# Scan stage of a two-layer metaformer: x1 added by a DMA after the states are turned, turns in one pass and earlier, softplus exponential in two halves

## The chip, the core and the metric

The kernel runs on one core of one Trainium2 chip, in float32. The metric is the device time of one launch in microseconds. The time of the kernel before is the median of three runs, 13239.91 us (13234.78 to 13243.13).

## The reference, cut to what matters

B = 64 images of 56x56 tokens (S = 3136) with C = 128 channels pass through two layers.

```python
x = x + window_attention(ln_c(x))                        # layer 0: x1
t = x1 + scan(ln_t(x1))                                  # layer 0: x2
#   Wx = batch_norm(ln_t(x1) @ W.T) over all tokens
#   step: y = sigmoid(wx_t + y @ V.T), 3136 steps in series, 64 images side by side
x = x2 + spectral_conv(ln_c(x2))                         # layer 1: x3
#   gates  = sigmoid(z @ Wf + bf + 2), sigmoid(z @ Wi + bi), delta = softplus(z @ Wd + bd) * 0.1
#   16 equal steps h = fg * (A*h) + delta*ig*(B*z), complex, elementwise
out = x3 + mixture_of_experts(ln_t(x3))
```

## The kernel before, in words

There are three stages: attention (one image after another, to about 5,200 us), the scan stage (`scan_phase`), and the experts. The scan stage works on all 64 images at once. In time it is cut into 25 chunks j of TF = 128 tokens (the last has 64). Each chunk has NO = 4 **slots** s = 0 to 3. In a slot three things go on beside each other, written out by hand in `slots()`:

- the recurrence of chunk j: 32 steps. A step is one product of TensorE (L1267, `vh` by the 64 states of the step before) and one tanh of ScalarE (L1136), in series. Every 8 steps the product with the inputs for 8 tokens (L1222) comes ahead of them;
- the gates of group oc: 16 images (OS) of chunk j-1. The states are turned (tokens to partitions) in four **quarters** q of 4 images by `turn_u`, copied from PSUM by `residual`, their moments are taken on VectorE (`statistics`, L935), the reciprocal root on POOL (L848 to L852), the normalization on ScalarE (L1152), the transposes on TensorE (L1254) and then 16 gate products (L1296) with two copies each (L1113, L1115). At the slot's end stand exponential (L1194) and logarithm (L1196) of the softplus, each with a table load where the function changes;
- the elementwise work of group o = oc-1 on VectorE (L1010 to L1071) with squares on ScalarE (L1157 to L1187).

Each slot has K = 32 positions k, one recurrence step each in a full chunk; TensorE and ScalarE run through them in order, and what stands at a position is done behind the step there. `turn_u` of the next group stands at k = 24, 26, 28, 30, the copies one later. A slot 0 has the turns of its own group at k = 0 to 3, since the chunk's states are complete only then; slot 3 has none for a next group. The normalization stands at k = 10 to 13 and the gates' copies from k = 17.

`turn_u` before makes one accumulation in PSUM of two things: x1, by a product with the identity (L1231), and half the state, by a product with half the identity `hident` (L1234). Both are float32 products, which take two passes, shown as two records. x1 comes from DRAM through `load_x1` on SP's queue into one of NX = 3 buffers X2. `residual` copies with a bias of 0.5. States are stored as 2y - 1, so x1 + half of one + 0.5 is x1 + y.

POOL's queue issues three accumulating transfers per group, all from SBUF to SBUF and 1 MB each: BX (L861), the state result (L817, `add_state`), and the input result (L825, `add_input`, one slot later, behind the landing of the state transfer). When that one has landed SP stores X2 to DRAM (L794). ScalarE's queue loads xh, the normalized x1, for the next chunk (L1086, `load_xq`).

The attention stage stores x1 and xh by images (L205, L207), in pieces of 512 bytes.

```python
for i in range(Q):
    w = pe.matmul(pY[0:tc, C * i:C * i + C], XU[c % 2][:, 0:tc, OS * s + Q * q + i], hident[:],
                  start=False, stop=True, skip_group_check=True)
w.then_inc(y_ps, 1)
```

## Time and profile before

| | |
|---|---|
| median of three runs | 13239.91 us |
| profiled execution, its own time | 13252.06 us |
| its span | 13250.1 us |
| PE / DVE / ACT / POOL busy | 76% / 77% / 69% / 39% |
| mean granted TensorE clock | 0.836 of full speed |
| DMA | 1215.93 MB in 1642383 packets |

The profile shows one execution. Shares of busy time are means over stages. The 40 slices of the page show the scan stage from the 17th to about the 34th, with VectorE at 8 tenths, TensorE at 7 and ScalarE at 6. The chain of work that ended last lies in the last stage and tells nothing of the scan. Within the scan I read the timeline of four slots. Busy times of neighbouring instructions overlap a little, so a stretch is best measured from start to start. Names: PEld is a weight load, SPq and ACTq are the queues of SP and ScalarE.

### The profile page before, as it was taken

What the parts mean: (1) busy time and instruction counts of PE and PEld (TensorE: products, weight loads), DVE (VectorE), ACT (ScalarE), POOL (GpSimd) and SP (SyncE); (2) the same over time, 40 slices, a digit from 0 to 9 for tenths busy, and PEclk for the clock granted to TensorE, in tenths of its full rate; (3) what the DMA queues carried; (4) which work ended last, traced back from release to release, by engine and by line L of the source; (5) the groups of instructions that cost most, each with busy time, mean ns of one, the idle gap of its engine ahead of it and who ended that gap; (6) DMA issues with size and microseconds to landing.
All of it is one profiled execution on the core that took longest, in us unless ns stands there. A gap on an engine that the chain in (4) does not pass through costs nothing. (4 is left out here: it accounts for less than half of the span.)

```text
span 13250.1 us, 228029 instructions
## 1 busy us (share of the span) xinstructions
PE 10057.1 (76%) x79510; PEld 7477.3 (56%) x79510; DVE 10189.2 (77%) x22622; ACT 9128.6 (69%) x21751; POOL 5150.9 (39%) x4755
## 2 busy tenths in 40 slices
PE   7888888888888886777777777777777777355544
PEld 5666666666666665555555555555555555133343
DVE  6777777777777774488888888888888889899910
ACT  6888888888888885466666666666666666476710
POOL 4444445444444443112212212222122122188866
PEclk9999999999999998677777777777777777677755
DMA  3333333333333332244444444444444444476544
GB/s 71 79 80 84 88 86 80 80 79 81 84 89 83 79 80 79 53 103 100 108 99 107 104 99 109 99 104 105 100 110 99 103 101 95 66 137 122 99 80 69
DMA packets 1642383, 1215.93 MB, mean 92 GB/s; under 512 B 65493, under 2 KB 1542168, under 8 KB 1603620
## 3 DMA queue, kind: packets, MB, share of 16 engines
q1 hardware_dynamic: 1345060, 756.57, 24.0%
q0 software_dynamic: 89088, 341.98, 14.0%
q10 hardware_dynamic: 207104, 102.79, 2.8%
q8 instruction: 649, 10.63, 0.3%
q14 instruction: 482, 3.95, 0.1%
HBM read 567.56 MB, written 325.32 MB: 67 GB/s over the span
## 5 line engine op out<-in xcount | busy, mean ns | idle before, releaser
L1267 PEld LDWEIGHTS s_pW<-s_XU,s_vh 128*128 128x128 f32 x6272 | 1414.0, 253 | 1884.9 <-ACT s_XU L1136 1574.5
L1267 PE MATMUL s_pW<-s_XU,s_vh 128*128 128x64 f32 x6272 | 1464.6, 325 | 1020.4 <-ACT s_XU L1136 1020.4
L1136 ACT ACTIVATE s_XU<-s_pW 128x64 f32<-128x64 f32 x3136 | 717.9, 229 | 1947.2 <-PE s_pW L1267 1927.7
L1296 PE MATMUL s_pG<-s_wg,s_XNT 128*128 128x384 f32 (+1 forms) x3200 | 1507.8, 560 | 15.4 <-ACT s_Z L1115 15.4
L409 ACT ACTIVATE KB<-pV,qkb 32x392 f32<-32x392 f32 x2048 | 1188.2, 580 | 25.7 <-PE pV L499 1.9
L249 POOL TENSOR_TENSOR SS<-SS,mx 128x784 f32<-128x784 f32 x512 | 768.7, 1501 | 805.7 <-DVE mx L342 805.5
L817 POOL DMA_DIRECT2D s_X<-s_f x100 | 87.1, 871 | 2190.4 <-DVE s_f L1067 2120.0
L1234 PEld LDWEIGHTS s_pY<-s_hident,s_XU 128*128 128x128 f32 (+1 forms) x3200 | 750.8, 305 | 174.4 <-issue 126.2
L257 POOL TENSOR_TENSOR XR<-XR,pbias 112x512 f32<-112x512 f32 x448 | 570.6, 1274 | 648.2 <-DMA XR<-in_x_dram 648.2
L461 ACT ACTIVATE XH<-XR,nm,rs 112x128 f32<-112x128 f32 x1792 | 731.3, 482 | 90.5 <-POOL nm L268 82.0
L507 PE MATMUL pS<-KB,QT 128*64 128x196 f32 x8192 | 793.3, 336 | 0.0
L529 PE MATMUL pV<-wq,XT 128*49 128x64 f32 x16384 | 564.6, 222 | 249.3 <-ACT KB L409 248.9
L507 PEld LDWEIGHTS pS<-KB,QT 128*64 128x64 f32 x8192 | 545.0, 137 | 352.8 <-issue 286.0
L353 DVE RECIPROCAL rc<-pO 128x16 f32<-128x16 f32 x512 | 131.3, 256 | 793.3 <-PE pO L550 793.3
L1152 ACT ACTIVATE s_f<-s_X,s_nmr,s_rst 128x128 f32<-128x128 f32 (+1 forms) x1600 | 652.9, 485 | 121.8 <-POOL s_nmr L852 121.7
L550 PE MATMUL pO<-Vb,PT 128*64 128x66 f32 x16384 | 591.5, 225 | 168.4 <-DVE gram L347 164.6
L1234 PE MATMUL s_pY<-s_hident,s_XU 128*128 128x128 f32 (+1 forms) x3200 | 716.8, 369 | 0.0
L529 PEld LDWEIGHTS pV<-wq,XT 128*49 128x49 f32 x16384 | 489.1, 124 | 368.7 <-ACT KB L409 368.2
L861 POOL DMA_DIRECT2D s_BX<-s_Dl x100 | 90.6, 906 | 1519.5 <-DVE s_Dl L929 1488.9
L1222 PE MATMUL s_pW<-s_XU,s_ws 128*128 128x512 f32 x784 | 671.1, 953 | 1.2 <-ACT s_XU L1096 1.2
L550 PEld LDWEIGHTS pO<-Vb,PT 128*64 128x64 f32 x16384 | 522.2, 137 | 256.9 <-DVE gram L347 217.9
L1663 PE MATMUL e_pT<-e_ident,e_X 112*128 112x112 f32 x1792 | 307.4, 335 | 443.9 <-ACT e_X L1599 288.6
(263 smaller groups left out, 30132.9 us busy)
## 6 DMA issues: line engine op xcount, KB each, us to landing
XL<-in_x_dram SPq DMA_DIRECT2D x64, 1568.0 KB, 12.4
XR<-in_x_dram SPq DMA_DIRECT2D x64, 1568.0 KB, 18.0
x_dram<-XR SPq DMA_DIRECT2D x64, 1568.0 KB, 8.0
xh_dram<-XH SPq DMA_DIRECT2D x64, 1568.0 KB, 8.1
e_X<-out_dram SPq DMA_DIRECT2D x64, 1568.0 KB, 16.1
s_XQ<-xh_dram ACTq DMA_DIRECT2D x384, 256.0 KB, 3.3
s_BX<-s_Dl POOLq DMA_DIRECT2D x96, 1024.0 KB, 7.0
s_X<-s_f POOLq DMA_DIRECT2D x96, 1024.0 KB, 7.0
```

The costliest lines, as they stand in the source:

```text
L249: pool.tensor_tensor(sv[:], sv[:], mx[wi % 2][:].unsqueeze(2).broadcast_to([P, 16, L]), ALU.subtract).then_inc(s_sub, 1)
L409: i = act.activation(KB[par][r, :, h, :], pV[r, 0:NW * L].rearrange("c (w l) -> c w l", l=L), ACT.Identity, bias=qkb[r, 1:2])
L461: i = act.activation(XH[q.par][:, n0, 0:C], XR[q.par][:, n0, :], ACT.Identity, bias=nm2[:, k, t:t + 1], scale=rs2[:, k, t:t + 1])
L507: i = pe.matmul(pS[64 * s:64 * s + 64, p // 2, (p % 2) * NH * L:(p % 2 + 1) * NH * L], QT[par][:, w * L:w * L + 64], KB[par][:, w, :, :].r ...
L529: i = pe.matmul(pV[64 * o:64 * o + L, 64 * w:64 * w + 64], XT[im.par][:, wi, w, :], wq[:, 2 * C:3 * C].rearrange("c (a b d) -> c a b d", a ...
L550: i = pe.matmul(pO[64 * s:64 * s + 64, hp, 66 * p:66 * p + 66], PT[par][:, p, hp, 64 * s:64 * s + 64], Vb[par][:, w, hp, :], start=True, s ...
L1136: act.activation(XU[j % 2][:, t, :], pW[t // R % 2][:, B * (t % R):B * (t % R) + B], ACT.Tanh, scale=0.5).then_inc(u_sb, 1)
L1152: w = act.activation(XN[0:tc, i, :], X2[oc % NX][0:tc, i, :], ACT.Identity, bias=nmr[0:tc, i:i + 1], scale=rst[0:tc, i:i + 1])
L1222: pe.matmul(pW[r % 2][:, 0:R * B], ws[:], XU[j % 2][:, R * r:R * r + R, :].rearrange("c t b -> c (t b)"), start=True, stop=False, skip_gro ...
L1234: w = pe.matmul(pY[0:tc, C * i:C * i + C], XU[c % 2][:, 0:tc, OS * s + Q * q + i], hident[:], start=False, stop=True, skip_group_check=True)
L1267: pe.matmul(pW[t // R % 2][:, B * (t % R):B * (t % R) + B], vh[:], before, start=False, stop=True, skip_group_check=True).then_inc(z_ps, 1)
L1296: pe.matmul(pG[i % 3][0:tc, 0:3 * C], XNT[:, i, 0:tc], wg[:], start=True, stop=True).then_inc(g_ps, 1)
```

## The change

Of the attention stage: x1 and xh are stored with the token as the outer dimension and the image as the second, so that 16 images of a token lie together (8 KB), and neighbouring tokens 32 KB apart.

Of the scan stage:

- `turn_u` is now four transposes of the states into PSUM, without x1. `hident` goes. The copy `residual` multiplies by 0.5 and adds 0.5. It waits for the store that last used the buffer.
- x1 is added to X2 afterwards by a transfer on POOL's queue from DRAM, `add_x1`, a fourth accumulating transfer per group. SP's loads go. `statistics` waits for its landing. For the groups of slots 1 to 3 it is issued in the slot before, between the BX transfer and the state transfer; for that of slot 0 in slot 0 itself, behind the input transfer of the group before.
- The turns of the next group move from k = 24, 26, 28, 30 to k = 17, 19, 21, 23, the copies from k = 25, 27, 29, 31 to k = 18, 20, 22, 24.
- The exponential is made of two halves, of 8 images each: the first at k = 29, the second at the old place.
- xh is loaded in pieces of 2 KB.

```diff
@@ -60,6 +60,11 @@
 def tokens_of(dram, b):
 
     return dram[bass.ds(b, 1)].rearrange("a (n r) w c -> (a r w) n c", r=2)
+
+
+def token_rows(dram, b):
+
+    return dram[:, b, :].rearrange("(n t) c -> t n c", t=T)
 
 
 PIECES = 1
...
@@ -202,9 +207,9 @@
                 if prev:
                     q = m.step(-1)
                     wait(sp, x1_sb, m.idx * NG)
-                    sp.dma_start(tokens_of(x1_d, q.idx), XR[q.par][:]).then_inc(x1_st[q.par], 16)
+                    sp.dma_start(token_rows(x1_d, q.idx), XR[q.par][:]).then_inc(x1_st[q.par], 16)
                     wait(sp, xh_sb, m.idx * NG)
-                    sp.dma_start(tokens_of(xh_d, q.idx), XH[q.par][:, :, 0:C]).then_inc(xh_st[q.par], 16)
+                    sp.dma_start(token_rows(xh_d, q.idx), XH[q.par][:, :, 0:C]).then_inc(xh_st[q.par], 16)
 
             bodies(body, sp)
             for i in range(2):
...
@@ -716,8 +720,9 @@
         cst = sem("cst"); ini = sem("ini"); dch = sem("dch"); pch = sem("pch"); mmc = sem("mmc")
         ready = sem("ready"); bf_d = sem("bf_d"); fold_ps = sem("fold_ps"); fold_d = sem("fold_d")
         xq_ld = [sem(f"xq_ld{i}") for i in range(2)]
-        x2_ld = [sem(f"x2_ld{i}") for i in range(NX)]
-        x3_st = sem("x3_st"); first_added = sem("first_added"); both_added = sem("both_added")
+        x1_added = [sem(f"x1_added{i}") for i in range(2)]
+        x3_st = [sem(f"x3_st{i}") for i in range(2)]
+        first_added = sem("first_added"); both_added = sem("both_added")
         d_ld = sem("d_ld"); d_ps = sem("d_ps")
         xt_ps = sem("xt_ps"); xt_sb = sem("xt_sb")
         w_ps = sem("w_ps"); z_ps = sem("z_ps"); u_sb = sem("u_sb")
...
@@ -758,6 +763,9 @@
 
         def tokens(dram, b0, n, j):
             return dram[b0:b0 + n, j * TF:j * TF + size(j), :].rearrange("b t c -> t b c")
+
+        def rows_of(dram, b0, n, j):
+            return dram[j * TF:j * TF + size(j), b0:b0 + n, :].rearrange("t b c -> t (b c)")
 
         @block.sync
         def _(sp):
...
@@ -775,15 +783,7 @@
                 sp.dma_start(kern[64:64 + L, o:o + HC], im).then_inc(cst, 16)
                 sp.dma_start(kern[64:64 + L, o + HC:o + 2 * HC], re).then_inc(cst, 16)
 
-            def load_x1(o):
-                c, s = divmod(o, NO)
-                wait(sp, x3_st, (o - NX + 1) * 16)
-                sp.dma_start(X2[o % NX][0:size(c)], tokens(x1_d, OS * s, OS, c)).then_inc(x2_ld[o % NX], 16)
-
-            load_x1(0)
             for j, s, oc, o, scan, prep in slots():
-                if oc is not None and oc + 1 < NGR:
-                    load_x1(oc + 1)
                 if scan and s == 1:
                     wait(sp, d_ps, j)
                     for n, a, e, at in pieces(j):
...
@@ -791,8 +791,9 @@
                 if o is not None:
                     c, s_ = divmod(o, NO)
                     sp.wait_ge(both_added, (o + 1) * 16)
-                    sp.dma_start(tokens(x3_d, OS * s_, OS, c), X2[o % NX][0:size(c)]).then_inc(x3_st, 16)
-            sp.wait_ge(x3_st, NGR * 16)
+                    sp.dma_start(tokens(x3_d, OS * s_, OS, c), X2[o % NX][0:size(c)]).then_inc(x3_st[o % 2], 16)
+            for i in range(2):
+                sp.wait_ge(x3_st[i], NGR // 2 * 16)
 
         @block.gpsimd
         def _(pool):
...
@@ -810,6 +811,13 @@
             pool.wait_ge(dch, 5)
             pool.tensor_tensor(fld[4], fld[3], nhalf[:, 0:C], ALU.pow).then_inc(pch, 1)
 
+            def add_x1(o):
+
+                c, s_ = divmod(o, NO)
+                pool.wait_ge(x2_d, o * NQ + NQ)
+                pool.dma_start(X2[o % NX][0:size(c)].rearrange("t b c -> t (b c)"), rows_of(x1_d, OS * s_, OS, c),
+                               accum_op=ALU.add).then_inc(x1_added[o % 2], 16)
+
             def add_state(o):
 
                 n = size(o // NO)
...
@@ -829,6 +837,8 @@
             for j, s, oc, o, scan, prep in slots():
                 if o is not None and o >= 1:
                     add_input(o - 1)
+                if oc is not None and s == 0:
+                    add_x1(oc)
                 if scan and s == NO - 2:
                     tj = size(j)
                     pool.wait_ge(raw_d, j + 1)
...
@@ -860,6 +870,8 @@
                     pool.wait_ge(bp, oc + 1)
                     pool.dma_start(BX[0:tc].rearrange("t r b c -> t (r b c)"), Dl[0:tc].rearrange("t r b c -> t (r b c)"),
                                    accum_op=ALU.add).then_inc(bx_d, 16)
+                if oc is not None and s + 1 < NO:
+                    add_x1(oc + 1)
                 if o is not None:
                     add_state(o)
             add_input(NGR - 1)
...
@@ -929,7 +940,7 @@
                 dve.tensor_tensor(Dl[0:tc], of[:, ::-1], by(C), ALU.mult).then_inc(part_sem, 1)
 
             def statistics(oc, tc):
-                dve.wait_ge(x2_d, oc * NQ + NQ)
+                dve.wait_ge(x1_added[oc % 2], (oc // 2 + 1) * 16)
                 wait(dve, ag_d, oc)
                 for i in range(OS):
                     w = dve.bn_stats(st[0:tc, i, :], X2[oc % NX][0:tc, i, :])
...
@@ -1083,7 +1094,7 @@
 
                 j, b = divmod(i, NO * NQ)
                 if j < NCH:
-                    act.dma_start(XQ[i % 2][0:size(j)], tokens(xh_d, Q * b, Q, j)).then_inc(xq_ld[i % 2], 16)
+                    act.dma_start(XQ[i % 2][0:size(j)].rearrange("t b c -> t (b c)"), rows_of(xh_d, Q * b, Q, j)).then_inc(xq_ld[i % 2], 16)
 
             def keep_turned(j, s, q):
 
...
@@ -1102,8 +1113,10 @@
 
                 tc = size(oc // NO)
                 act.wait_ge(y_ps, oc * NQ + q + 1)
+                if q == 0 and oc >= NX:
+                    act.wait_ge(x3_st[(oc - NX) % 2], ((oc - NX) // 2 + 1) * 16)
                 act.activation(X2[oc % NX][0:tc, Q * q:Q * q + Q, :].rearrange("t b c -> t (b c)"), pY[0:tc, :], ACT.Identity,
-                               bias=cols[0:tc, 1:2]).then_inc(x2_d, 1)
+                               bias=cols[0:tc, 1:2], scale=0.5).then_inc(x2_d, 1)
 
             def gate(oc, tc, i):
                 act.wait_ge(g_ps, oc * OS + i + 1)
...
@@ -1114,6 +1127,13 @@
                                scale=0.5)
                 act.copy(Z[0:tc, :, i, :], bank[:, 2 * C:3 * C].rearrange("t (r c) -> t r c", r=2)).then_inc(g_sb, 1)
 
+            def exponential(oc, tc, first, last):
+
+                act.wait_ge(g_sb, oc * OS + last)
+                if first == 0:
+                    act.wait_ge(bx_d, (oc + 1) * 16)
+                act.activation(Dl[0:tc, :, first:last], Z[0:tc, :, first:last], ACT.Exp).then_inc(sp_d, 1)
+
             for i in range(2):
                 load_xq(i)
 
...
@@ -1137,8 +1157,8 @@
                                            scale=0.5).then_inc(u_sb, 1)
                     if conv and s == 0 and k in (1, 2, 3, 4):
                         residual(oc, k - 1)
-                    if conv and s + 1 < NO and k in (25, 27, 29, 31):
-                        residual(oc + 1, (k - 25) // 2)
+                    if conv and s + 1 < NO and k in (18, 20, 22, 24):
+                        residual(oc + 1, (k - 18) // 2)
                     if prep and k in (1, 4, 7, 10):
                         keep_turned(j, s, k // 3)
                     if conv and 10 <= k < 10 + NQ:
...
@@ -1187,12 +1207,12 @@
                         act.activation(t1, t2, ACT.Square, bias=cols[0:tm, 2:3]).then_inc(am, 1)
                     if conv and k > K - OS:
                         gate(oc, tc, k - (K - OS) - 1)
+                    if conv and k == K - 3:
+                        exponential(oc, tc, 0, OS // 2)
                 if conv:
                     gate(oc, tc, OS - 1)
-                    act.wait_ge(g_sb, oc * OS + OS)
-                    act.wait_ge(bx_d, (oc + 1) * 16)
-                    act.activation(Dl[0:tc], Z[0:tc], ACT.Exp).then_inc(sp_d, 1)
-                    act.wait_ge(sp_d, oc * 2 + 1)
+                    exponential(oc, tc, OS // 2, OS)
+                    act.wait_ge(sp_d, oc * 3 + 2)
                     act.activation(Dl[0:tc], Dl[0:tc], ACT.Ln, bias=cols[0:tc, 0:1]).then_inc(sp_d, 1)
 
         @block.tensor
...
@@ -1226,13 +1246,8 @@
                 c, s = divmod(oc, NO)
                 tc = size(c)
                 wait(pe, x2_d, oc * NQ + q)
-                if q == 0:
-                    pe.wait_ge(x2_ld[oc % NX], (oc // NX + 1) * 16)
-                pe.matmul(pY[0:tc, :], ident[0:tc, 0:tc], X2[oc % NX][0:tc, Q * q:Q * q + Q, :].rearrange("t b c -> t (b c)"),
-                          start=True, stop=False, skip_group_check=True)
                 for i in range(Q):
-                    w = pe.matmul(pY[0:tc, C * i:C * i + C], XU[c % 2][:, 0:tc, OS * s + Q * q + i], hident[:],
-                                  start=False, stop=True, skip_group_check=True)
+                    w = pe.transpose(pY[0:tc, C * i:C * i + C], XU[c % 2][:, 0:tc, OS * s + Q * q + i], ident[:])
                 w.then_inc(y_ps, 1)
 
             def turn_inputs(j, s, q, oc):
...
@@ -1277,8 +1292,8 @@
                         if k == 0:
                             pe.wait_ge(u_sb, (j - 1) * TF + tc)
                         turn_u(oc, k)
-                    if conv and s + 1 < NO and k in (24, 26, 28, 30):
-                        turn_u(oc + 1, (k - 24) // 2)
+                    if conv and s + 1 < NO and k in (17, 19, 21, 23):
+                        turn_u(oc + 1, (k - 17) // 2)
                     if prep and k in (0, 3, 6, 9):
                         turn_inputs(j, s, k // 3, oc)
                     if conv and 11 <= k < 11 + NQ:
...
@@ -1709,9 +1724,10 @@
     with ExitStack() as ctx:
 
         gram = ctx.enter_context(nc.sbuf_tensor("gram", [C, C + 1], F32))
+        x1_d, xh_d = (d.rearrange("b h w c -> (b h w) c").rearrange("(s b) c -> s b c", b=B) for d in (x1_d, xh_d))
         attention_phase(nc, B, A["x"], A["w_qkvT"], A["qkv_bias"], A["w_projT"], A["proj_bias"], A["rel_table"],
                         A["mask"], A["ident"], A["ones"], x1_d, xh_d, gram)
-        scan_phase(nc, B, x1_d.rearrange("b h w c -> b (h w) c"), xh_d.rearrange("b h w c -> b (h w) c"), gram,
+        scan_phase(nc, B, x1_d, xh_d, gram,
                    A["w_ffnT"], A["v_ffnT"], A["gamma"], A["beta"], A["w_gates"], A["b_gates"], A["dft"],
                    (A["A_re"], A["A_im"]), (A["B_re"], A["B_im"]), A["ident"], A["ones"], out)
         tv_d = nc.dram_tensor("tv_dram", [2, B, E, TOPK // 2], F32, kind="Internal").ap()
```

TensorE, the later part of a slot with turns, before. s_pY<-s_X,s_ident is x1 by the identity, s_pY<-s_hident,s_XU the states, s_pG a gate, s_pW<-s_XU,s_vh a step.

```order
L1231 MATMUL s_pY<-s_X,s_ident 128x512
L1234 MATMUL s_pY<-s_hident,s_XU 128x128 x4
L1296 MATMUL s_pG<-s_wg,s_XNT 128x384
L1267 MATMUL s_pW<-s_XU,s_vh 128x64
L1296 MATMUL s_pG<-s_wg,s_XNT 128x384
L1267 MATMUL s_pW<-s_XU,s_vh 128x64
L1231 MATMUL s_pY<-s_X,s_ident 128x512
L1234 MATMUL s_pY<-s_hident,s_XU 128x128 x4
L1296 MATMUL s_pG<-s_wg,s_XNT 128x384
L1267 MATMUL s_pW<-s_XU,s_vh 128x64
L1296 MATMUL s_pG<-s_wg,s_XNT 128x384
L1267 MATMUL s_pW<-s_XU,s_vh 128x64
```

The same engine after the change, from the step of k = 17 on.

```order
L1282 MATMUL s_pW<-s_XU,s_vh 128x64
L1250 MATMUL s_pY<-s_ident,s_XU 128x128 x4
L1311 MATMUL s_pG<-s_wg,s_XNT 128x384
L1282 MATMUL s_pW<-s_XU,s_vh 128x64
L1242 MATMUL s_pW<-s_XU,s_ws 128x512
L1311 MATMUL s_pG<-s_wg,s_XNT 128x384
L1282 MATMUL s_pW<-s_XU,s_vh 128x64
L1250 MATMUL s_pY<-s_ident,s_XU 128x128 x4
L1311 MATMUL s_pG<-s_wg,s_XNT 128x384
L1282 MATMUL s_pW<-s_XU,s_vh 128x64
L1311 MATMUL s_pG<-s_wg,s_XNT 128x384
L1282 MATMUL s_pW<-s_XU,s_vh 128x64
```

Before, a turn stands among the last eight gates; now it stands among the first eight, and x1's product is not there.

POOL from the end of a slot 3 into slot 0, before (s_BX<-s_Dl is the BX transfer, s_X<-s_f the state's, s_X<-s_Wv the input's).

```order
L861 DMA s_BX<-s_Dl 128x2048
L817 DMA s_X<-s_f 128x2048
L825 DMA s_X<-s_Wv 128x2048
L848 TENSOR_TENSOR s_rst<-s_var,s_epst 128x16
L850 TENSOR_TENSOR s_rst<-s_rst,s_nhalf 128x16
L852 TENSOR_TENSOR s_nmr<-s_mean,s_rst 128x16
```

The same place after the change.

```order
L862 TENSOR_TENSOR s_nmr<-s_mean,s_rst 128x16
L871 DMA s_BX<-s_Dl 128x2048
L825 DMA s_X<-s_f 128x2048
L833 DMA s_X<-s_Wv 128x2048
L818 DMA s_X<-x_dram 128x2048
L858 TENSOR_TENSOR s_rst<-s_var,s_epst 128x16
L860 TENSOR_TENSOR s_rst<-s_rst,s_nhalf 128x16
L862 TENSOR_TENSOR s_nmr<-s_mean,s_rst 128x16
```

At the turn from slot 3 to slot 0, x1's transfer (s_X<-x_dram) stands behind the input transfer and ahead of the reciprocal roots; in the other slots it stands ahead of the state transfer.

ScalarE at a slot's end, after the change (L1135 is the exponential, L1156 the step's tanh).

```order
L1156 ACTIVATE s_XU<-s_pW 128x64
L1126 ACTIVATE s_TG<-s_pG 128x4x64
L1128 COPY s_Z<-s_pG 128x2x64
L1135 ACTIVATE s_Dl<-s_Z 128x2x512
L1156 ACTIVATE s_XU<-s_pW 128x64
L1126 ACTIVATE s_TG<-s_pG 128x4x64
L1128 COPY s_Z<-s_pG 128x2x64
L1156 ACTIVATE s_XU<-s_pW 128x64
L1126 ACTIVATE s_TG<-s_pG 128x4x64
L1128 COPY s_Z<-s_pG 128x2x64
L1126 ACTIVATE s_TG<-s_pG 128x4x64
L1128 COPY s_Z<-s_pG 128x2x64
L1135 ACTIVATE s_Dl<-s_Z 128x2x512
L1216 ACT_TABLE_LOAD
```

The first half of the exponential stands ahead of the tanh of k = 30.

## Rows read from the trace of the kernel before

**Rows 1.** Windows, scan stage: engines' busy time with counts, granted clock, DMA share, GB/s.

```profile
5000.00:11400.00 6400.00, 4805.53 (x19398) 3463.39 (x19399) 5239.44 (x5770) 4140.21 (x10445) 1440.06 (x852) 0.77 0.42 98
```

**Rows 2.** Line L1194 on ScalarE: count, ns min/median/max, first and last start.

```profile
L1194 ACT ACTIVATE s_Dl<-s_Z x100: 1909/1910/1917, 5493.8 to 11499.2; 128x2048 f32<-128x2048 f32 x96, 64x2048 f32<-64x2048 f32 x4
```

**Rows 3.** Timeline, ScalarE, slots' ends: start us, duration us, instruction [idle before <-releaser].

```profile
8010.81 1.91 ACT L1194 ACTIVATE s_Dl<-s_Z 128x2048 f32<-128x2048 f32 x1
...
8072.10 1.91 ACT L1194 ACTIVATE s_Dl<-s_Z 128x2048 f32<-128x2048 f32 x1
...
8121.62 1.91 ACT L1194 ACTIVATE s_Dl<-s_Z 128x2048 f32<-128x2048 f32 x1
...
8195.83 1.91 ACT L1194 ACTIVATE s_Dl<-s_Z 128x2048 f32<-128x2048 f32 x1
...
8256.61 1.91 ACT L1194 ACTIVATE s_Dl<-s_Z 128x2048 f32<-128x2048 f32 x1
```

**Rows 4.** Timeline, TensorE: one quarter turned, and four transposes of inputs.

```profile
8005.48 1.13 PE L1231 MATMUL s_pY<-s_X,s_ident 128*128 128x512 f32 x2
...
8006.02 2.04 PEld L1234 LDWEIGHTS s_pY<-s_hident,s_XU 128*128 128x128 f32 x8 [0.24 <-issue]
...
8007.97 0.32 PEld L1296 LDWEIGHTS s_pG<-s_wg,s_XNT 128*128 128x128 f32 x2
...
8010.05 0.57 PEld L1247 LDWEIGHTS s_pX<-s_ident,s_XQ 128*128 128x128 f32 x4
```

**Rows 5.** Tile s_XU: weight loads of the states, ns min/median/max.

```profile
L1234 PEld LDWEIGHTS s_pY<-s_hident,s_XU x3200: 184/313/338, 5429.8 to 11452.0; 128*128 128x128 f32 x181, 128*64 128x64 f32 x8
```

**Rows 6.** Windows of slot 3 around the clock's rise.

```profile
8104.00:8108.00 4.00, 4.00 (x8) 2.18 (x8) 4.00 (x4) 1.31 (x6) 0.90 (x1) 0.51 0.66 133
8108.00:8112.00 4.00, 3.67 (x17) 2.33 (x16) 1.51 (x2) 2.96 (x11) 0.00 (x0) 1.00 0.66 135
```

**Rows 7.** Timeline, VectorE, slot 3 and the start of slot 0.

```profile
8071.28 3.19 DVE L935 BATCH_NORM_STATS2 s_st<-s_X 128x6 f32<-128x128 f32 x16 [0.66 <-ACT s_X L1105]
...
8075.32 1.23 DVE L1010 TENSOR_TENSOR s_f<-s_TG 128x1024 f32<-128x1024 f32 x1
...
8099.37 2.29 DVE L928 TENSOR_TENSOR s_BX<-s_f,s_par_b 128x2048 f32<-128x2048 f32 x1 [2.33 <-ACT s_f L1152]
...
8110.89 1.23 DVE L1053 SCALAR_TENSOR_TENSOR s_f<-s_f,s_d 128x1024 f32<-128x1024 f32 x1 [2.49 <-ACT s_f L1183]
...
8113.23 1.23 DVE L1055 SCALAR_TENSOR_TENSOR s_t<-s_t,s_d 128x1024 f32<-128x1024 f32 x1 [1.11 <-ACT s_t L1187]
...
8129.65 1.23 DVE L1010 TENSOR_TENSOR s_f<-s_TG 128x1024 f32<-128x1024 f32 x1
...
8143.47 3.19 DVE L935 BATCH_NORM_STATS2 s_st<-s_X 128x6 f32<-128x128 f32 x16 [2.34 <-ACT s_X L1105]
```

**Rows 8.** Timeline, POOL and SP's queue, slot 0.

```profile
8135.69 0.86 POOL L825 DMA_DIRECT2D s_X<-s_Wv  x1 [7.35 <-DMA s_X<-s_f]
...
8142.64 0.37 SPq L794 DMA_DIRECT2D out_dram<-s_X  x1
...
8154.88 0.67 POOL L852 TENSOR_TENSOR s_nmr<-s_mean,s_rst 128x16 f32<-128x16 f32 x1
```

**Rows 9.** Window of slot 0 while POOL's input transfer runs.

```profile
8137.00:8139.00 2.00, 1.33 (x8) 1.20 (x7) 1.97 (x2) 0.63 (x2) 0.00 (x0) 1.00 0.98 197
```

**Rows 10.** DMA queues of the page: packets, MB, share of 16 engines.

```profile
q1 hardware_dynamic: 1345060, 756.57, 24.0%
q0 software_dynamic: 89088, 341.98, 14.0%
```

**Rows 11.** Timeline, slot 0: ScalarE's normalization and who reads its result.

```profile
8155.58 1.65 ACT L1152 ACTIVATE s_f<-s_X,s_nmr,s_rst 128x128 f32<-128x128 f32 x4 [3.91 <-POOL s_nmr L852]
...
8162.78 2.29 DVE L928 TENSOR_TENSOR s_BX<-s_f,s_par_b 128x2048 f32<-128x2048 f32 x1 [5.08 <-ACT s_f L1152]
```

**Rows 12.** DMA issues of the page: KB each, median us to landing.

```profile
x_dram<-XR SPq DMA_DIRECT2D x64, 1568.0 KB, 8.0
```

4 lines of the change are left out of this document (1 added, 3 removed).

## The prediction

> **What bounds the kernel now.** I read the busy times of the scan stage first. Between 5000 and 11400 us VectorE is busy 5239 us of 6400, TensorE 4806, ScalarE 4140, and TensorE has a mean clock of 0.77 [rows 1]. No engine is full, so the order between them counts. The exponential of the softplus stands once at each slot's end and serves as a mark: 100 of them from 5493.8 to 11499.2 us, 60.7 us from one to the next [rows 2]. In the chunk I read, one after the other, the slots take 61.3, 49.5, 74.2 and 60.8 us [rows 3]. These are s = 2, 3, 0 and 1, 245.8 us together. Slot 3 turns no states for a next group; slot 0 turns its own and the next group's.
>
> **TensorE's part.** One quarter of the states is turned from 8005.48, when the identity product on x begins, to 8007.97, when the next gate weights are loaded [rows 4]: 2.5 us at full clock. Four of them and what they hold up are the 11.8 us between slots 2 and 3 [rows 3]. The change drops the identity product and one of the two passes. The eight weight loads of the states take 2.04 us [rows 4], so four take 1.0 us; the longest single one is 338 ns [rows 5], so 1.3 us at half clock. Both ends of the price of a new quarter stand in rows: 0.57 us, as the four transposes of contiguous data take [rows 4], and 1.35. I take 1.0 at full clock, since the states still lie apart in memory.
>
> **Where they go.** They move from k = 24 to 30 to k = 17 to 23. There ScalarE has two squares (k = 20 and 22), behind which the turns at k = 21 and 23 lie, and now the four copies from PSUM of about 0.57 us as well. Unhidden are the turns at 17 and 19 (1.3 and 1.0) and the copies at 20, 22, 24 and part of that at 18: 4.7 us a slot. The least is 2.3 (the two turns alone), the most 6.6 (four turns and four copies).
>
> **The exponential.** 1.91 us [rows 3] become two of about 1 us. The second saves 0.95 us at the slot's end. The first stands on ScalarE in front of the step of k = 30, and that step waits for it; about 0.6 comes back. Net gain 0.35 us a slot, between 0 and 0.95.
>
> **So TensorE and ScalarE alone** would allow 49.5 - 0.35 = 49.15 us in slot 3, and 53.9 in slots 1 and 2, together 157.
>
> **VectorE is late next.** In slot 3 it goes from 8075.32 to 8129.65 with waits of 2.33, 2.49 and 1.11 us: 48.4 us of work. Statistics of a group take 4.05 (8071.28 to 8075.32) [rows 7]. Beside that I allow 1.0 and 2.4 us for the spectrum's operations in slots 1 to 2 and 2. For slots 1 to 3 that is 3 x 48.4 + 3 x 4.05 + 3.4 = 160.8 us of work. Some 2 us of waits for ScalarE's squares stay in each slot, 166.8. VectorE comes into slot 1 about 6 us behind the mark and leaves slot 3 about 8 behind (8129.65 against 8121.62 before [rows 3, 7]), so 2.2 of it fall outside: 164.6 us for three slots that took 171.6. **Gain 7.0**, at most 10.5 (without waits), at least 2.
>
> **Slot 0 pays.** Its statistics needed only ScalarE's copy and began 21.9 us after the mark (8143.47), after a wait of 2.34 us [rows 7]. Now they need the added x1. Its transfer can start only when the copies are done, about 16.4 us after the mark (0.95 from the tail and 1.5 from each of three turns, 5.4 earlier than before). But POOL issues it behind the input transfer of the group before. That was issued 14.1 us after the mark (8135.69) [rows 8] and lands about 7 us later, at 21. VectorE now comes into the slot about 0.6 us later than before: 21.7. Do the two run at the same time? During the earlier one all 16 DMA engines were busy (0.98) [rows 9]. The software queue took 14.0% of 16 engines' span for 342 MB: 5.4 us per MB; its three transfers per group carry 300 MB in all, so 6.2 us per transfer. The hardware queue took 24.0% for 757 MB, 4.2 us per MB [rows 10]. Behind the first, x1 lands at 21.7 + 6.2 = 27.9 at the earliest. As the store of the finished group starts then too (8142.64, 21.0 after the mark [rows 8]), at 21.7 + 6.2 + 4.2 = 32.1 at the latest, or 33 with a load of xh. I take 31.5, the shared end, since both are issued at the same moment. The Trainium skill, "DMA: Bandwidth & Descriptors", section on queues, rings and completion order, says that each DMA engine goes round-robin between the queue rows that have work; by that the shared end is the right one, by a strict order of arrival it would be 27.9.
>
> From there the old chain follows: from the start of statistics to the end of POOL's last operation (8155.55) 12.1 us [rows 7, 8]; ScalarE's normalization 7.2 (8155.58 to 8162.78) [rows 11]; and from there to the slot's end 33.0 [rows 3], now 33.0 - 11.3 (turns; 0.5 of the 11.8 are slot 2's spectrum) + 4.7 + 0.6 = 27.0. New length 31.5 + 12.1 + 7.2 + 27.0 = 77.8 us instead of 74.2. **Loss 3.6.** ScalarE waited 3.91 us there for POOL [rows 11]; it will wait some 19 (5.4 earlier there, 9.7 later served), with TensorE idle.
>
> **Costed at nothing.** SP's loads of x1 go; none was waited for. Loads of xh in longer pieces were hidden. The attention stage stores x1 and xh with neighbouring tokens 32 KB apart. One store of 1568 KB lands in 8.0 us [rows 12] and an image takes some 80; it would have to take nearly ten times as long to be seen. If that cover were gone, each us beyond would cost 64. POOL's wait for the copies of k = 24 stands ahead of its state transfer, which VectorE releases later anyway, and delays nothing.
>
> **Sum.** +3.6 - 7.0 = -3.4 us per chunk, 25 chunks: -85 us. The profiled execution took 13252.1 us, 12 more than the median of 13239.9; from it 13167, from the median 13155. What a measurement can tell from no change is 0.2%, 26 us or 1.1 us per chunk.
>
> **Rivals.**
> 1. *The late x1 decides (slower).* One mechanism: x1 queues behind another transfer ahead of slot 0's statistics. Each us of its landing costs 25 us. At 31.5 the kernel gains 85; at 34.9 it breaks even; from 36 on it is slower by over 0.2%. At 39, if store and xh loads come first and the transfer from DRAM has a longer way, it is 13155 + 7.5 x 25 = 13340. For it: the engines are full at that place [rows 9]. Against: the bytes queued there give 33. Chance 0.24; a shortfall of VectorE's gain to its least, 2, gives the same sign and is counted here.
> 2. *x1 slips through.* It lands at 27.9, and VectorE's waits shrink to nothing: -3.6 - 3.5 = -7.1 more per chunk, 12980. For it: transfers may overlap their fixed part. Chance 0.20.
> 3. *The clock stays low.* In slot 3 the granted clock is 0.51 from 8104 to 8108, with 8 products started, and 1.00 from 8108 to 8112, with 17 [rows 6]: half the rate is about 1 us per step and gate. It rose after a row of gate products; now transposes with the idle array between them stand there, and slot 0 idles longer ahead. If the full clock came four steps later in slots 0 to 2, slot 0 would lose 4 us, and VectorE, the later one in the others, would hide about half: +8 per chunk, 13355. The Trainium skill, "TensorE: Matmul & The Clock Gate", section on the transpose in TensorE, says that transposes do not count as busy for the clock in the way products do; by it this rival would come out. Against: slot 3 has no turns at all and reaches 1.00 by its gates alone, so I give 0.08.
> 4. *It evens out.* Gains of VectorE's slots and slot 0's loss are equal within 1.1: 13240. Chance 0.12.
>
> **Chances.** Forecast 0.36, rivals 0.24, 0.20, 0.08, 0.12. Faster takes the forecast and the second: 0.56; slower the first and third, less a little at their near edge: 0.30; the rest 0.14. The range leaves out half of the second rival's far end and the tops of the first and third: 13000 to 13320. The forecast's own range is 13080 to 13210.
>
> **What would show it.** Marks of slots 1 and 2 about 55 to 57 us apart, slot 3 about 53, slot 0 about 78. In slot 0 statistics wait for the x1 transfer and begin about 31 us after the mark, and ScalarE's normalization waits about 19 us for POOL. The turn of a quarter takes 1.0 to 1.3 us. Statistics of the other slots wait for nothing. The attention stage has the same length. I am wrong if slot 0 is not longer, or if slots 1 to 3 sum to under 160 or over 169 us.

## The result, and the profile after

The changed kernel takes **13162.5 us**, the median of four runs (13158.25 to 13164.23), against 13239.6 for the kernel before in four runs beside them: a ratio of 0.9941, 95% interval 0.9925 to 0.9957. That is 77 us less. Forecast were 13155 and a range of 13000 to 13320.

The slots' ends can be read as before. The first view is ScalarE's timeline of the kernel after: the second half of the exponential at each slot's end (start us, duration us, instruction).

```profile
7962.83 1.06 ACT L1135 ACTIVATE s_Dl<-s_Z 128x1024 f32<-128x1024 f32 x1
...
8023.98 1.06 ACT L1135 ACTIVATE s_Dl<-s_Z 128x1024 f32<-128x1024 f32 x1
...
8076.71 1.11 ACT L1135 ACTIVATE s_Dl<-s_Z 128x1024 f32<-128x1024 f32 x1
...
8150.46 1.06 ACT L1135 ACTIVATE s_Dl<-s_Z 128x1024 f32<-128x1024 f32 x1
...
8205.02 1.06 ACT L1135 ACTIVATE s_Dl<-s_Z 128x1024 f32<-128x1024 f32 x1
```

| slot | before [rows 3] | forecast | after |
|---|---|---|---|
| 2 | 61.3 | 55 to 57 | 61.2 |
| 3 | 49.5 | 53 | 52.7 |
| 0 | 74.2 | 77.8 | 73.7 |
| 1 | 60.8 | 55 to 57 | 54.6 |
| 1 to 3 together | 171.6 | 164.6 | 168.4 |
| chunk | 245.8 | 242.4 | 242.2 |

The chunk came out within 0.2 us of the forecast, by two errors of about 4 us that cancel: slot 0 was shorter than forecast, and slot 2 gained nothing. The chunk that I read is a usual one: the medians over all chunks, slots 0 to 3, are 74.2, 60.7, 61.3 and 49.5 us before and 73.7, 54.3, 61.0 and 52.7 after. From the first mark to the last the scan took 6005.4 us before [rows 2] and 5926.9 after (5495.3 to 11422.2, by the second halves), 78.5 less. The two profiled executions differ by more, 13250.1 and 13156.4 us of span. The rest lies behind the last mark, where the execution of before took 1750.9 us and this one 1734.2; the profiles of three variants (the late turns, the new layout alone, the early turns alone) have 1728.9 to 1733.5 there, so it was that one execution of before that was long, and not the change.

The next view is the windows of the kernel after, the scan stage as in [rows 1] and then slots 2, 3, 0 and 1. The columns are those of [rows 1]: length, PE, PEld, DVE, ACT and POOL busy, granted clock, DMA share, GB/s.

```profile
5000.00:11400.00 6400.00, 4167.50 (x17204) 2939.09 (x17204) 5320.54 (x5869) 4227.06 (x10652) 1642.33 (x966) 0.69 0.46 99
...
8023.98:8076.71 52.73, 35.28 (x131) 24.52 (x131) 52.08 (x61) 38.63 (x100) 8.11 (x6) 0.71 0.44 100
8076.71:8150.46 73.75, 43.65 (x175) 31.20 (x173) 53.63 (x53) 43.50 (x109) 12.09 (x8) 0.68 0.46 100
8150.46:8205.02 54.56, 40.62 (x153) 28.74 (x153) 51.80 (x52) 40.92 (x105) 9.73 (x7) 0.69 0.54 117
7962.83:8023.98 61.15, 41.21 (x157) 28.87 (x155) 53.17 (x56) 41.38 (x105) 31.19 (x13) 0.69 0.48 103
```

TensorE has lost 640 us of busy time in the stage (4805.5 to 4167.5) and the kernel only 77: TensorE is not what sets the slots now. In slot 3 VectorE is busy 52.08 of 52.73 us, and in slot 1 51.80 of 54.56. Slots 0 and 2 are the ones with idle time on VectorE, 20 and 8 us. The timeline of VectorE after, slot 3 and the start of slot 0, answers to [rows 7]:

```profile
8036.83 1.23 DVE L1021 TENSOR_TENSOR s_f<-s_TG 128x1024 f32<-128x1024 f32 x1
...
8084.98 1.23 DVE L1021 TENSOR_TENSOR s_f<-s_TG 128x1024 f32<-128x1024 f32 x1
...
8105.30 3.19 DVE L946 BATCH_NORM_STATS2 s_st<-s_X 128x6 f32<-128x128 f32 x16 [8.84 <-DMA s_X<-x_dram]
...
8124.60 2.29 DVE L939 TENSOR_TENSOR s_BX<-s_f,s_par_b 128x2048 f32<-128x2048 f32 x1 [5.09 <-ACT s_f L1172]
```

From 8036.83 to 8084.98 there is no bracket at all on VectorE: 48.15 us of pure work, where it had three waits before. Then the statistics of slot 0 wait 8.84 us for the landing of x1, 28.6 us after the mark at 8076.71. What was queued there is in the timeline of POOL, SP and ScalarE, slot 0 after, which answers to [rows 8] and [rows 11]:

```profile
8090.95 0.86 POOL L833 DMA_DIRECT2D s_X<-s_Wv  x1 [7.29 <-DMA s_X<-s_f]
8092.25 0.87 POOL L818 DMA_DIRECT2D s_X<-x_dram  x1 [0.43 <-ACT s_X L1118]
...
8099.41 0.37 SPq L794 DMA_DIRECT2D out_dram<-s_X  x1
...
8116.70 0.67 POOL L862 TENSOR_TENSOR s_nmr<-s_mean,s_rst 128x16 f32<-128x16 f32 x1
...
8117.40 1.65 ACT L1172 ACTIVATE s_f<-s_X,s_nmr,s_rst 128x128 f32<-128x128 f32 x4 [17.01 <-POOL s_nmr L862]
```

The input transfer is issued at 8090.95, x1 1.3 us behind it, the store 7.2 us later. ScalarE waits 17.0 us for POOL. x1 has moved to the software queue, which carries 444.75 MB now instead of 341.98 [rows 10]. From the page's DMA part (the second line is to be read against [rows 12]):

```profile
q0 software_dynamic: 103232, 444.75, 18.7%
...
x_dram<-XR SPq DMA_DIRECT2D x64, 1568.0 KB, 8.1
...
s_XQ<-xh_dram ACTq DMA_DIRECT2D x384, 256.0 KB, 4.5
```

### The profile page after: what moved, and what is told of

The parts are those of the page before. It is cut to its first block and busy times, and to the rows that moved or that the text cites. A ratio compares the mean times of both kernels' runs of the same rounds, so it can differ in the third digit from the quotient of the medians.

```text
span 13156.4 us, 223254 instructions
## 1 busy us (share of the span) xinstructions
PE 9385.1 (71%) x77110; PEld 6941.7 (53%) x77110; DVE 10185.1 (77%) x22621; ACT 9159.4 (70%) x21851; POOL 5332.7 (41%) x4855
## 3 DMA queue, kind: packets, MB, share of 16 engines
q0 software_dynamic: 103232, 444.75, 18.7%
## 5 line engine op out<-in xcount | busy, mean ns | idle before, releaser
L1282 PEld LDWEIGHTS s_pW<-s_XU,s_vh 128*128 128x128 f32 x6272 | 1451.6, 263 | 2039.1 <-ACT s_XU L1156 1758.7
L1282 PE MATMUL s_pW<-s_XU,s_vh 128*128 128x64 f32 x6272 | 1523.5, 336 | 1132.1 <-ACT s_XU L1156 1117.2
L1156 ACT ACTIVATE s_XU<-s_pW 128x64 f32<-128x64 f32 x3136 | 715.0, 228 | 1179.0 <-PE s_pW L1282 1146.8
L1269 PE MATMUL s_pN<-s_ident,s_f 128*128 128x128 f32 (+1 forms) x800 | 211.0, 418 | 826.1 <-issue 437.9
L437 ACT COPY Vb<-pV 49x512 f32<-49x512 f32 x1024 | 597.6, 584 | 61.7 <-PE pV L534 3.0
L1311 PEld LDWEIGHTS s_pG<-s_wg,s_XNT 128*128 128x128 f32 (+1 forms) x3200 | 561.3, 212 | 141.2 <-issue 111.2
L1126 ACT ACTIVATE s_TG<-s_pG 128x256 f32<-128x256 f32 (+1 forms) x1600 | 621.1, 388 | 9.7 <-DVE s_Wv L1046 2.4
```

What stands on the lines that cost most here:

```text
L1126: act.activation(TG[0:tc, :, i, :], bank[:, 0:2 * C].rearrange("t (r c) -> t r c", r=4), ACT.Tanh, scale=0.5)
L1156: act.activation(XU[j % 2][:, t, :], pW[t // R % 2][:, B * (t % R):B * (t % R) + B], ACT.Tanh, scale=0.5).then_inc(u_sb, 1)
L1282: pe.matmul(pW[t // R % 2][:, B * (t % R):B * (t % R) + B], vh[:], before, start=False, stop=True, skip_group_check=True).then_inc(z_ps, 1)
L1311: pe.matmul(pG[i % 3][0:tc, 0:3 * C], XNT[:, i, 0:tc], wg[:], start=True, stop=True).then_inc(g_ps, 1)
```

## Experiments

Slot lengths below are read from each run's marks as above. All kernels start from the changed one but two, which start from before (the early turns alone and the new layout alone); each ratio is against the kernel before, run beside it. The runs were made in several sets, in which the kernel before took 13231.5, 13234.9 and 13239.6 us; a difference between two variants given in us can be off by such an amount. Each trace is that of one execution.

### Slot 0: is it the late x1, and what makes it late?

**Without x1 in slot 0** (`add_x1` is not issued for the groups of slot 0, whose statistics wait for ScalarE's copies instead):

```diff
-                if oc is not None and s == 0:
-                    add_x1(oc)
...
-                dve.wait_ge(x1_added[oc % 2], (oc // 2 + 1) * 16)
+                if oc % NO == 0:
+                    dve.wait_ge(x2_d, oc * NQ + NQ)
+                else:
+                    dve.wait_ge(x1_added[oc % 2], (oc // 2 + 1 if oc % 2 else oc // NO + 1) * 16)
```

> The changed kernel without x1 for the groups of slot 0: its transfer is left out there and statistics wait for the copies alone (a quarter of the groups lacks x1). In the changed kernel statistics of slot 0 waited 8.84 us for that transfer. Theory (slot 0 pays for the late x1): slot 0 becomes some 9 us shorter, 25 times, 12940 us. Rival (VectorE is the bound over all four slots, so that a later wait takes the place): under 100 us less, 13070 or more.

12917.4 us, ratio 0.9761 (0.9745 to 0.9778). Slot 0 takes 64.3 us, and its statistics start 18.9 us after the mark. The late x1 costs 245 us, and 9.5 us in the slot 0 that I read: much more than the 3.6 that I had put down as slot 0's loss, because without it slot 0 would have gained 10.

**Slot 0 the old way** (`load_x1` on SP's queue, x1's identity product and the two-pass products in slot 0 alone; other slots as changed):

```diff
...
+                if s == 0:
+                    if q == 0:
+                        pe.wait_ge(x2_ld, (c + 1) * 16)
+                    pe.matmul(pY[0:tc, :], ident[0:tc, 0:tc], X2[oc % NX][0:tc, Q * q:Q * q + Q, :].rearrange("t b c -> t (b c)"),
+                              start=True, stop=False, skip_group_check=True)
                 for i in range(Q):
-                    w = pe.transpose(pY[0:tc, C * i:C * i + C], XU[c % 2][:, 0:tc, OS * s + Q * q + i], ident[:])
+                    if s == 0:
+                        w = pe.matmul(pY[0:tc, C * i:C * i + C], XU[c % 2][:, 0:tc, OS * s + Q * q + i], hident[:],
+                                      start=False, stop=True, skip_group_check=True)
+                    else:
+                        w = pe.transpose(pY[0:tc, C * i:C * i + C], XU[c % 2][:, 0:tc, OS * s + Q * q + i], ident[:])
...
```

> Groups of slot 0 get x1 as before the change (SP loads it, product with the identity, two passes for the states), the other three as after it. Theory: in slot 0 the four old turns put the last copy at about 21 us after the mark (21.8 before the change, less the shorter tail) instead of x1's landing at 28.6; 7.6 us less, 25 times, 12970 us. Rival (what counts in slot 0 is TensorE's own work and clock): the old turns cost there what the wait did, 13160.

12939.4 us, ratio 0.9777 (0.9761 to 0.9793). Slot 0 takes 64.6 us, its statistics start 20.6 us after the mark and wait 0.78 us. So slot 0 is as short with the old, dearer turns as with the new ones and no x1 (64.3): there it is not TensorE that counts but when x1 has arrived.

**x1 ahead of the input transfer** on POOL's queue in slot 0:

```diff
-                if o is not None and o >= 1:
-                    add_input(o - 1)
                 if oc is not None and s == 0:
                     add_x1(oc)
+                if o is not None and o >= 1:
+                    add_input(o - 1)
```

> In slot 0 POOL issues x1's transfer ahead of the input transfer of the group before, not behind it. Theory (x1 stands in a full queue): the copies are done about 15.5 us after the mark, x1 lands alone at about 23 to 24 instead of 28.6, statistics begin 5 us earlier, 13040 us. Rival (transfers in flight share the engines whatever their order): x1 lands where it did, 13160. The input transfer lands later, at about 29, which statistics cover.

12934.1 us, ratio 0.9775 (0.9759 to 0.9792). The two lines' order alone is worth 228 us, and the result is within 17 us of the kernel that has no x1 there at all. The expected 13040 was too high. Timeline of VectorE and POOL in this kernel's slot 0, whose mark is at 7977.46:

```profile
8001.07 3.19 DVE L946 BATCH_NORM_STATS2 s_st<-s_X 128x6 f32<-128x128 f32 x16 [3.80 <-DMA s_X<-x_dram]
...
8006.80 2.29 DVE L939 TENSOR_TENSOR s_Wv<-s_IN,s_par_a 128x2048 f32<-128x2048 f32 x1 [1.62 <-DMA s_X<-s_Wv]
```

```profile
8005.26 0.21 POOL L858 TENSOR_TENSOR s_rst<-s_var,s_epst 128x16 f32<-128x16 f32 x1 [10.48 <-DVE s_var L85]
8005.55 2.93 POOL L860 TENSOR_TENSOR s_rst<-s_rst,s_nhalf 128x16 f32<-128x16 f32 x1
8008.56 0.61 POOL L862 TENSOR_TENSOR s_nmr<-s_mean,s_rst 128x16 f32<-128x16 f32 x1
```

x1 lands 23.6 us after the mark instead of 28.6, the 5.0 us expected. The other 4 us are seen at POOL: its three operations end 3.9 us after they began, and VectorE now waits 1.62 us for the input transfer beside them. In the changed kernel they run beside VectorE's work and take 7.9 us (8109.49 to 8117.37), as they did before (8147.67 to 8155.55), and as they do in the run without x1, where VectorE does not wait there either. That the wait is what makes them short is read from these timelines and was not tried by itself.

**The store held back.** SP waits with the store of the finished group until slot 0's statistics are done. The first form had the group's number one off and held another slot's store, where nothing is late:

```diff
+                    if (o + 1) % NO == 0 and o + 1 < NGR:
+                        sp.wait_ge(ag_d, o + 2)
```

> In slot 0 SP stores the finished group only once the statistics are done, so that the store does not run beside x1's transfer. If the store and x1 share the engines, as I took it for the prediction: x1 lands at 27 instead of 28.6, up to 35 us less in all, 13130. If the order of arrival decides: no change, 13160.

13154.5 us, ratio 0.9942 (0.9925 to 0.9958): the same as the change. It decides nothing, and serves as a second measurement of it. The right form:

```diff
+                    if (o + 2) % NO == 0 and o + 2 < NGR:
+                        sp.wait_ge(ag_d, o + 3)
```

> The wait of e_hold stood one slot off and held no store of slot 0; here SP's store that falls in slot 0 is held until slot 0's statistics are done. If x1 and the store share the engines equally, x1 lands 3 to 4 us earlier than its 28.6 after the mark, 13070. If the earlier transfer keeps nearly all of the engines: under 1 us, 13150.

13146.3 us, ratio 0.9934 (0.9917 to 0.9950). Timeline of VectorE and SP's queue in slot 0 of this kernel, whose mark is at 8074.28:

```profile
8102.57 3.19 DVE L948 BATCH_NORM_STATS2 s_st<-s_X 128x6 f32<-128x128 f32 x16 [8.59 <-DMA s_X<-x_dram]
```

```profile
8106.75 0.37 SPq L796 DMA_DIRECT2D out_dram<-s_X  x1
```

The store is issued behind x1's landing now, and x1 lands 28.3 us after the mark instead of 28.6. So the store does not delay it. The packets of the kernel after show it too. First the queues between the store's issue and x1's landing (8099.41 to 8105.30), then from there to 8109.50 (packets, MB, share of 16 engines; q0 is POOL's, q1 SP's):

```profile
q0 software_dynamic: 125, 0.89, 77.3%
...
q1 hardware_dynamic: 128, 0.07, 4.1%
```

```profile
q1 hardware_dynamic: 1936, 0.98, 77.4%
```

Of the store's 2064 packets 128 run before x1 has landed, and 1936 after it. What delays x1 is the input transfer ahead of it on its own queue. The store, which waits for that transfer, is issued 22.7 us after the mark, and x1 lands 5.9 us behind that.

### Slot 2: why did it gain nothing?

**POOL's parameters of B behind the reciprocal root.** In slot 2 POOL also scales `par_b`, four small operations (L848 to L851), ahead of the root. The experiment moves them behind everything of that slot up to the magnitudes' root (L867 of the kernel after):

```diff
-                    pool.tensor_tensor(pb[:, 0:HC], rw[:, 2 * HC:3 * HC], twentieth[0:tj], ALU.mult)
...
                     pool.tensor_tensor(sa[0:tj], sa[0:tj], phalf[0:tj], ALU.pow).then_inc(mag_d, 1)
+                    pool.tensor_tensor(pb[:, 0:HC], rw[:, 2 * HC:3 * HC], twentieth[0:tj], ALU.mult)
...
```

> In slot 2 POOL's four products for par_b, 5.4 us there beside VectorE, move from ahead of the reciprocal roots to behind them; nothing needs par_b before the next chunk. Slot 2 took 61.2 us where I had forecast 57.0, and ScalarE waited 4.97 us there for POOL. Theory (POOL's queue is what holds slot 2): the wait goes, slot 2 takes 56 to 57 us, 13045. Rival (VectorE's own work and TensorE's half clock hold it): under 40 us less, 13120 or more.

13009.9 us, ratio 0.9832 (0.9816 to 0.9848): 153 us less than the change. Slot 2 takes 54.9 us instead of 61.2 (slots 3, 0 and 1 of the same chunk 54.0, 72.4 and 54.2). The cause can be read in three views. First the timeline of POOL before, slot 2, whose mark is at 8010.81:

```profile
8012.92 0.64 POOL L838 TENSOR_TENSOR s_par_b<-s_raw,s_twentieth 128x64 f32<-128x64 f32 x1
8013.63 0.38 POOL L839 TENSOR_SCALAR s_par_b<-s_raw 128x64 f32<-128x64 f32 x1
...
8015.66 1.15 POOL L848 TENSOR_TENSOR s_rst<-s_var,s_epst 128x16 f32<-128x16 f32 x1 [0.79 <-DVE s_var L80]
```

Then the same engine after, whose slot begins at 7962.83:

```profile
7975.33 0.85 POOL L833 DMA_DIRECT2D s_X<-s_Wv  x1 [7.31 <-DMA s_X<-s_f]
7975.89 0.84 POOL L848 TENSOR_TENSOR s_par_b<-s_raw,s_twentieth 128x64 f32<-128x64 f32 x1
7976.80 1.25 POOL L849 TENSOR_SCALAR s_par_b<-s_raw 128x64 f32<-128x64 f32 x1
7978.11 1.10 POOL L850 TENSOR_SCALAR s_par_b<-s_raw 128x64 f32<-128x64 f32 x1
7979.28 2.18 POOL L851 TENSOR_SCALAR s_par_b<-s_raw 128x64 f32<-128x64 f32 x1
7981.54 2.09 POOL L858 TENSOR_TENSOR s_rst<-s_var,s_epst 128x16 f32<-128x16 f32 x1
7983.71 4.97 POOL L860 TENSOR_TENSOR s_rst<-s_rst,s_nhalf 128x16 f32<-128x16 f32 x1
```

And VectorE beside it, of the kernel after:

```profile
7975.34 1.22 DVE L1022 SCALAR_TENSOR_TENSOR s_d<-s_TG,s_par_a 128x1024 f32<-128x1024 f32 x1
7976.47 1.34 DVE L1024 SCALAR_TENSOR_TENSOR s_f<-s_f,s_par_a 128x1024 f32<-128x1024 f32 x1
7977.74 1.25 DVE L1026 SCALAR_TENSOR_TENSOR s_d<-s_TG,s_d 128x1024 f32<-128x1024 f32 x1
7978.91 2.32 DVE L1028 SCALAR_TENSOR_TENSOR s_Dl<-s_Dl,s_Z 128x2048 f32<-128x2048 f32 x1
7981.26 2.29 DVE L1030 SCALAR_TENSOR_TENSOR s_Dl<-s_TG,s_Dl 128x2048 f32<-128x2048 f32 x1
```

Two things happen. VectorE is further behind the mark than before, and the state transfer waits for VectorE, the input transfer for the state transfer, and POOL stands in that wait: `par_b` starts 13.1 us after the mark instead of 2.1. And there it no longer runs beside the statistics (8011.47 to 8014.65 before) but beside VectorE's operations on two operands. Each POOL operation then ends 0.1 to 0.25 us behind the end of a VectorE operation: at 7976.73, 7978.05, 7979.21, 7981.46 and 7983.63, where VectorE's end at 7976.56, 7977.81, 7978.99, 7981.23 and 7983.55. One small operation costs what is left of the large one beside it: the four of `par_b` take 0.84, 1.25, 1.10 and 2.18 us instead of 0.64, 0.38, 0.37 and 0.37. The Trainium skill, "SBUF — State Buffer", section on the two separate sides, says that VectorE and GpSimd share a port pair under an exclusive lock held for a whole instruction, which a VectorE operation with two SBUF inputs takes against a GpSimd operation that reads SBUF; by that rule the trace agrees in each of the five ends. The root is ready 27.7 us after the mark instead of 11.7, and ScalarE, which is ready for it at 22.7, waits 4.97. ScalarE's squares come late then, and VectorE waits 7.5 us in all for ScalarE in that slot (1.55, 4.21 and 1.73). ScalarE's row, after:

```profile
7990.52 1.65 ACT L1172 ACTIVATE s_f<-s_X,s_nmr,s_rst 128x128 f32<-128x128 f32 x4 [4.97 <-POOL s_nmr L862]
```

**Both together**, x1 first and `par_b` last:

> e_swap and e_parb together. One took 228 us from the changed kernel, the other 152. If they act at two places of the chunk (slot 0's x1, slot 2's POOL queue) and VectorE has slack left, both gains stand: 12780. If VectorE's 212.8 us of work per chunk with its remaining waits now binds: 12830 or more.

**12822.7 us** (12817.32 to 12823.80), ratio 0.9682 (0.9666 to 0.9698): 3.2% under the kernel before and 340 us under the change, by the order of six instructions of POOL's queue. It is 41 us less than the sum of the two (228 + 153), and nearer to the second expectation, in which VectorE's work binds, than to the first. A chunk takes 227.0 us, slots 0 to 3 about 64.6, 54.3, 54.9 and 53.2 (means of two chunks), and VectorE is busy 5602.7 of 6400 us. In slot 0 it still waits 3.5 to 5.3 us for x1 in the chunks that I read.

### The turns: the place or the passes?

**One pass, old place** (turns back at k = 24, 26, 28, 30, copies one later):

> The turns of the next group go back to k = 24 to 30 and their copies to 25 to 31; one pass and x1 by transfer stay. My account: unhidden turns cost 4.0 us there against 4.7 at the new place, and x1 is issued some 7 us later, which VectorE, being behind, hides for the most part: 13160, at most 60 off. Rival (the earlier place is what made the gain): more than 100 us slower, 13260.

13222.7 us in ten runs, ratio 0.9992 (0.9982 to 1.0001): 60 us more than the change. Slots 2, 3, 0, 1 take 64.0, 51.6, 74.5 and 55.4. VectorE waits for x1 in nearly every slot now (waits of the window 5000 to 11400: us in all, times, longest):

```profile
DVE s_st L946 <- DMA s_X<-x_dram: 469.0, 94, 61.3
```

After the change it is 295.9 us in 26 waits, one of them the first of the scan with 60.7. On the other side VectorE waits less for ScalarE's squares here, 149.4 us in all against 298.3 after the change, and 226.7 against 172.5 for the normalization. From the old place to the new one these three sums change by -173, +149 and -54 us, -78 together, and the scan from first to last mark by -75 (6002.2 and 5926.9). So the earlier place does not pay through the squares, which it delays even with the cheap turn. By these waits it pays because the copies, and with them x1's transfer, come earlier.

**New place, two passes** (an ordinary product with the identity in place of the transpose):

```diff
-                    w = pe.transpose(pY[0:tc, C * i:C * i + C], XU[c % 2][:, 0:tc, OS * s + Q * q + i], ident[:])
+                    w = pe.matmul(pY[0:tc, C * i:C * i + C], XU[c % 2][:, 0:tc, OS * s + Q * q + i], ident[:], start=True,
+                                  stop=True, skip_group_check=True)
```

> The turns are ordinary two-pass products with the identity, no transposes; all else as changed. My account: 1.0 us more TensorE work per quarter, of which VectorE's lag hides about half in slots 1 and 2: 13200 to 13260. Rival (transposes leave the clock low and products raise it): the mean clock of the stage rises from 0.69 towards the 0.77 of before and the time stays or falls, 13160 or less.

13335.0 us, ratio 1.0076 (1.0059 to 1.0093): 172 us more than the change, and slower than before. A quarter's weight loads take 1.8 us of TensorE instead of 0.7 to 0.9, some 15 to 18 us more per chunk, of which 6.9 are seen. VectorE's waits for the two squares grow from 298.3 to 462.3 us, and its other waits change by less than 12: these 164 us are nearly the whole of the 172. The clock rises a little earlier with products in slot 1, 34.1 us after the mark instead of 37.2, but not in slots 0 and 3, and its mean over the stage is 0.71 instead of 0.69.

**Before, with the turns at k = 17 to 23 and nothing else:**

```diff
-                    if conv and s + 1 < NO and k in (25, 27, 29, 31):
-                        residual(oc + 1, (k - 25) // 2)
+                    if conv and s + 1 < NO and k in (18, 20, 22, 24):
+                        residual(oc + 1, (k - 18) // 2)
...
-                    if conv and s + 1 < NO and k in (24, 26, 28, 30):
-                        turn_u(oc + 1, (k - 24) // 2)
+                    if conv and s + 1 < NO and k in (17, 19, 21, 23):
+                        turn_u(oc + 1, (k - 17) // 2)
```

> The kernel before with the turns of the next group at k = 17 to 23 and nothing else. The turns of 2.5 us (3.7 at half clock) then cost about 3.7 at k = 17, 2.5 at 19, 1.4 each behind ScalarE's squares at 21 and 23 and a copy of 0.6: 9.6 instead of 11.8 us a slot, three slots a chunk: 13070 if all else follows, 13150 if VectorE takes half. Rival (the place makes no difference): 13235.

13385.1 us, ratio 1.0107 (1.0091 to 1.0124): 146 us slower than before. I had it faster by some 100; this is the largest miss of the study. The timeline of TensorE in this kernel shows a quarter at its new place:

```profile
8040.30 1.93 PE L1231 MATMUL s_pY<-s_X,s_ident 128*128 128x512 f32 x2
8042.06 1.81 PE L1234 MATMUL s_pY<-s_hident,s_XU 128*128 128x128 f32 x8
8043.71 0.81 PE L1296 MATMUL s_pG<-s_wg,s_XNT 128*128 128x384 f32 x2
```

It takes 3.4 us, with a mean granted clock of 0.75, where a quarter took 2.5 at full clock at the slot's end [rows 4], and it stands ahead of ScalarE's squares at k = 20 and 22. VectorE's waits for the two squares (same view as above):

```profile
DVE s_f L1053 <- ACT s_f L1183: 454.0, 72, 7.5
DVE s_t L1055 <- ACT s_t L1187: 235.4, 79, 3.7
```

Before they were 192.4 and 101.7 us. Slots 2, 3, 0, 1 take 65.1, 51.1, 71.9 and 61.2 in the chunk read, and the mean of a chunk between first and last mark is 248.4 against 242.6. So the early place pays 60 us in the changed kernel and costs 146 in the kernel before, and the cheap turn (with x1 by a transfer) at the old place gives 12 us, which the interval does not tell from nothing: only the two together bring something. The two kernels differ in more than the passes: only the changed one has an x1 transfer that the early place lets start sooner. That the squares carry the loss is read from the waits of this run and of the two-pass run, and was not tried by moving them.

### The small parts

**The exponential whole again:**

> The softplus exponential whole and at the slot's end, all else as changed. I costed the halves at 0.35 us gained per slot: 13162 to 13195. If the first half costs the step of k = 30 nothing: 0.95 us per slot, 13255. If it gives back all it saves: 13160.

13159.4 us, ratio 0.9935 (0.9918 to 0.9952): the halves give nothing. Slots 54.1, 61.0, 52.7 and 73.8 for 1, 2, 3 and 0.

**Before with the new layout alone:**

> The kernel before with x1 and xh stored and loaded in the new layout alone. Costed at nothing: 13235, within 26. Rival: stores 32 KB apart hold up the attention stage, 13270 or more; or longer pieces of xh spare TensorE its 23 us of waits for them, 13205.

13249.3 us in ten runs, ratio 1.0006 (0.9997 to 1.0016): nothing that can be measured, at most 21 us. The stores land in 8.1 us, loads of xh in 3.0.

## Why the prediction was right, and which of its steps were not

By its own signs the prediction fails in one: it called itself wrong if slot 0 was not longer, and slot 0 takes 73.7 us where it took 74.2. Slots 1 to 3 take 168.4 us, just inside the 160 to 169 that it allowed. So the whole time was forecast well, and its parts were not.

**Slots 1 and 3: as reckoned.** 54.6 and 52.7 us against 55 and 53. The step "VectorE is late next" held to a quarter of a microsecond: 48.4 us of work forecast, 48.15 seen between the two L1021 in slot 3. The 2 us of waits for squares that I left in every slot are 2.4 in slot 1, none in slot 3, and 5.9 in slot 2, for the reason below. With 1.55 us for the normalization in slot 2, VectorE's waits in the three slots come to 9.9 us instead of 6, which is the whole of their 3.8 us over the forecast.

**Slot 0's landing of x1: 31.5 forecast, 28.6 measured.** The failed step is the choice of the shared end. My strict order gave 27.9 (21.7 for the input transfer and 6.2 for x1), and that was nearly right: 22.7 and 5.9 were measured. The run with the store held back shows why: x1 lands at 28.3 with no store beside it. The Trainium skill, "DMA: Bandwidth & Descriptors", section on queues, rings and completion order, says that a DMA engine goes round-robin between the queue rows that have work; by that I had expected equal shares and some microseconds for the store, and this trace does not agree: only 128 of the store's 2064 packets ran before x1 had landed. Why they stood back is open. The rest of the chain was right: from statistics to POOL's last operation 12.1 us forecast and 12.1 measured, normalization 7.2 and 7.2, from there to the mark 27.0 and 25.9. So 28.6 + 12.1 + 7.2 + 25.9 = 73.8. ScalarE waited 17.0 us (19 forecast).

**Slot 2: 55 to 57 forecast, 61.2 measured.** The step that failed stands in "VectorE is late next": I let VectorE fall behind and asked only what that costs VectorE. I did not follow what it releases: state transfer, input transfer, POOL's queue, `par_b`, the root, ScalarE. Nor did I price POOL's operations by what runs beside them, though the trace of before had both prices for the first operation of the root, 1.15 us in slot 2 and 2.19 in slot 0. The experiment on `par_b` shows the cause by its size: 6.3 us of slot 2. In the forecast's terms, the 7.0 us that slots 1 to 3 were to gain came to 3.2, near the least of 2.

**The sum.** -3.4 us per chunk forecast, -3.6 read, -3.2 as the mean between first and last mark. It was right by cancellation, and that is luck: +3.8 in slots 1 to 3 (all of it slot 2) against -4.1 in slot 0. Neither of the rivals on x1 came true alone. Rival 2 had the landing right, but not the time, since slot 2 took back what it would have brought. Rival 1 had the mechanism, x1 queued behind another transfer, but not its size: it never reached the 34.9 us from which it decides. What I did not see is how much slot 0 had to gain without it: 9.9 us (74.2 to 64.3), where I reckoned 6.0 for the turns, since the statistics start 3.0 us earlier too (18.9 against 21.9 us after the mark).

**The quarter's price: 1.0 us at full clock and 1.3 at half forecast, 0.7 and 0.9 measured.** Two quarters of slot 0 in the timeline of the kernel after, the first at a granted clock of 0.50 and the second at 1.00, and the next gate's weights:

```profile
8128.98 0.89 PEld L1250 LDWEIGHTS s_pY<-s_ident,s_XU 128*128 128x128 f32 x4
...
8133.98 0.69 PEld L1250 LDWEIGHTS s_pY<-s_ident,s_XU 128*128 128x128 f32 x4
8134.56 0.34 PEld L1311 LDWEIGHTS s_pG<-s_wg,s_XNT 128*128 128x128 f32 x2
```

The 1.3 us came from four times the longest single load, but neighbouring loads overlap. From start to start a quarter at full clock takes 0.58 us, where it took 2.5 before: it is the other end that I had named, 0.57, that came out. The copies from PSUM take 0.68 us before and after (median), not the 0.57 that I took, and with my 0.57 the unhidden part comes to 4.6 at most, not 4.7. None of this shows in the slots, likely because VectorE and x1 set them.

**The clock: later, by 8 us in two slots, but as a result and not as a cause.** Its mean in slots 0, 1 and 2 fell from 0.82, 0.80 and 0.78 to 0.68, 0.69 and 0.69, and rose from 0.69 to 0.71 in slot 3, which has no turns. Windows of 1 us in slot 1 after (mark 8150.46) show the rise:

```profile
8186.46:8187.46 1.00, 1.00 (x2) 0.39 (x2) 1.00 (x2) 1.00 (x4) 0.18 (x1) 0.50 0.00 0
8187.46:8188.46 1.00, 1.00 (x4) 0.40 (x3) 1.00 (x2) 0.08 (x1) 0.74 (x1) 0.88 0.00 0
```

It goes from 1.2 to 2.4 GHz 37.2 us after the mark. The last rise of each slot, in us from its mark:

| slot | before | after |
|---|---|---|
| 0 | 47.8 | 56.4 |
| 1 | 35.0 | 37.2 |
| 2 | 35.7 | 44.0 |
| 3 | 35.8 | 37.4 |

Rival 3 asked for a rise some four steps later in slots 0 to 2. In slots 0 and 2 it is over 8 us later, but there everything behind the late normalization is late: without x1 in slot 0 the rise comes at 47.1, and with `par_b` moved it comes at 37.0 in slot 2. What is left, 2.2 us or less, did not cost what the rival asked: from slot 0's normalization to its mark it took 25.9 us, and the forecast without a later clock had 27.0. The Trainium skill, "TensorE: Matmul & The Clock Gate", section on the transpose in TensorE, says that transposes do not count as busy in the way products do; the trace agrees in direction in the means, 0.69 with transposes and 0.71 with products in the same places. The rise itself comes 3.1 us earlier with products in slot 1, 0.8 in slot 2, and slightly later in slots 3 and 0. As the products also take twice as many passes, this run cannot tell the kind of the product from the number of passes. They cost 172 us all the same.

**The halves of the exponential: 0.35 us a slot forecast, nothing measured.** The likely reason is that in slots that VectorE or the late x1 sets, an earlier end on ScalarE is idle time; no run shows it by itself. **The layout and the loads: nothing, as costed.** Loads of xh got slower, 4.5 us instead of 3.3 in the page, but 3.0 with the layout alone, so the layout is not the cause. TensorE's weight loads wait for them 32.6 us in 36 times instead of 23.3 in 14, at most 1.7 us each.

**What "the place" is worth.** I costed passes and place together by what lies on TensorE and ScalarE. The runs say that the two cannot be costed apart: 60 us gained by the place in the changed kernel, 146 lost in the kernel before. By the waits above two things have to be weighed. The turns push the squares back: 395 us more of waiting in the kernel before, 149 in the changed one. And in the changed one VectorE waits less for x1 and for the normalization, by 173 and 54 us. I had put neither into the prediction's price for the place. A kernel with early turns whose x1 transfer is held to its old time would part them; it was not run.

## What to carry to other kernels

When an engine becomes the late one, follow what its last instruction releases, queue by queue, until something is waited for again; here that chain through POOL was worth twice the whole change (153 us against 77). Before an accumulating transfer takes the place of a product, look at what stands ahead of it on its own queue: the order of two issues was worth 228 us. And take a small POOL operation's price from a row where VectorE does what it will do beside it.

## What was not expected of the hardware

- Small POOL operations on 128x64 took 0.37 to 0.64 us beside VectorE's statistics and 0.84 to 2.18 us beside its operations on two operands; the root's three took 7.9 us beside VectorE's work and 3.9 us where VectorE was partly idle.
- Two 1 MB transfers issued 1.3 us apart on POOL's queue were done 14.4 us after the first was issued; a 1 MB store that the other queue issued in between took nothing that shows from them (28.6 us against 28.3 from the mark), and 1936 of its 2064 packets ran behind them.
- Stores in 512-byte pieces with neighbouring tokens 32 KB apart landed as fast as before, 8.1 us against 8.0.
